# A graph kernel on one NeuronCore: setup work in another order, and entry groups two batches apart

## What is computed

```
h = relu(layernorm(x))
h = tanh(h @ W_in + b_in)
deg = clip(segment_sum(1, dst), 1)
for _ in range(12):
    agg = segment_sum(h[src], dst) / deg
    diff = tanh(gelu(agg @ W1 + b1) @ W2 + b2)
    h = h + (diff - relu(clearance) * h) * 0.5
x = x + h
h = relu(layernorm(x))
h = relu(gcn_conv(h, src + loops, dst + loops, G1, gb1))
x = x + gcn_conv(h, src + loops, dst + loops, G2, gb2)
```

## Time and profile before

| | |
|---|---|
| median of 3 runs | 1400.75 us (1399.76 to 1405.07) |
| the profiled execution | 1402.87 us |
| its span | 1400.7 us |
| mean granted clock | 0.965 |
| VectorE, ScalarE busy in the span | 405.4, 319.1 us |
| first regular window product, last one | 41.18, 152.93 us |
| first matmul of the edge sums | 156.66 us |

### The profile page before, as it was taken

The page is one execution under the profiler, slowest core; times in us unless marked ns, Lnnn a source line. Parts: engine busy times, 40 slices in busy tenths (PEclk is TensorE's granted clock), DMA queues, the critical chain, the costliest instruction groups (busy, mean ns, idle before and its releaser), DMA issues. The chain is left out here.

```text
span 1400.7 us, 17327 instructions
## 1 busy us (share of the span) xinstructions
PE 1305.5 (93%) x7202; PEld 737.1 (53%) x7202; DVE 405.4 (29%) x802; ACT 319.1 (23%) x452; POOL 34.5 (2%) x48
## 2 busy tenths in 40 slices
PE   2898899999999999999999999999999999759898
PEld 1777555455554554645546455454564555524445
DVE  6779412213022130121301213012130121382412
ACT  1678412213012130121301213012130121300100
POOL 3600000000000000000000000000000000000000
PEclk7689999999999999999999999999999999969999
DMA  3000200000000000000000000000000000130011
GB/s 92 1 1 0 59 1 0 0 0 0 0 0 0 0 0 0 0 0 0 0 0 0 0 0 0 0 0 0 0 0 0 0 0 0 46 92 1 20 43 31
DMA packets 23670, 13.57 MB, mean 10 GB/s; under 512 B 6075, under 2 KB 23253, under 8 KB 23392
## 3 DMA queue, kind: packets, MB, share of 16 engines
q1 hardware_dynamic: 21550, 12.28, 3.3%
q10 hardware_dynamic: 1698, 0.66, 0.2%
q0 software_dynamic: 400, 0.33, 0.1%
HBM read 9.42 MB, written 3.44 MB: 9 GB/s over the span
## 5 line engine op out<-in xcount | busy, mean ns | idle before, releaser
L619 PE MATMUL ps<-adj,hi 128*128 128x512 f16 (+2 forms) x2450 | 816.1, 354 | 29.9 <-DVE lo L1125 25.2
L621 PE MATMUL ps<-adj,lo 128*128 128x512 f16 (+2 forms) x2352 | 797.7, 353 | 0.0
L619 PEld LDWEIGHTS ps<-adj,hi 128*128 128x128 f16 x2450 | 238.6, 98 | 280.6 <-issue 46.5
L621 PEld LDWEIGHTS ps<-adj,lo 128*128 128x128 f16 x2352 | 229.6, 98 | 243.8 <-issue 24.2
L1040 DVE TENSOR_TENSOR ps<-ps,bias 128x512 f32<-128x512 f32 (+1 forms) x84 | 53.7, 640 | 547.9 <-PE ps L641 547.9
L782 ACT ACTIVATE scratch<-ps 128x512 f32<-128x512 f32 (+1 forms) x84 | 46.3, 551 | 655.4 <-DVE ps L1040 655.4
L632 PE MATMUL ps<-scratch,w 128*128 128x512 f32 (+2 forms) x336 | 141.0, 542 | 14.9 <-ACT scratch L774 14.9
L774 ACT ACTIVATE scratch<-ps,b1c,cols 128x512 f32<-128x512 f32 (+2 forms) x168 | 113.3, 721 | 156.9 <-PE ps L632 155.9
L641 PEld LDWEIGHTS ps<-w,scratch 128*128 128x128 f32 x1200 | 143.3, 192 | 6.3
L641 PE MATMUL ps<-w,scratch 128*128 128x128 f32 x1200 | 146.1, 275 | 0.0
L1033 DVE TENSOR_TENSOR scratch<-ps,scratch 128x512 f32<-128x512 f32 (+2 forms) x84 | 51.9, 618 | 189.8 <-PE ps L632 132.6
(11 more groups left out here) (123 smaller groups left out, 210.4 us busy)
## 6 DMA issues: line engine op xcount, KB each, us to landing
scratch<-rdeg_scratch SPq DMA_DIRECT2D x1, 1562.5 KB
scratch<-dinv_scratch SPq DMA_DIRECT2D x1, 1562.5 KB, 7.2
state<-in_x_dram SPq DMA_DIRECT2D x5, 256.0 KB, 6.7
scratch<-in_x_dram SPq DMA_DIRECT2D x5, 256.0 KB, 4.4
x_scratch<-state SPq DMA_DIRECT2D x5, 256.0 KB
state<-x_scratch SPq DMA_DIRECT2D x5, 256.0 KB
out_dram<-state SPq DMA_DIRECT2D x5, 256.0 KB
adj<-adj SPq DMA_DIRECT2D x1, 390.6 KB, 4.0
```

The costliest lines, as they stand in the source:

```text
L619: nc.tensor.matmul(bank, hi[:, k, :], adj[:, k, c0:c0 + n], start=(at == 0), stop=False)
L621: mm = nc.tensor.matmul(bank, lo[:, k, :], adj[:, k, c0:c0 + n], start=False, stop=(k == K_ORDER[-1][0]))
```

## The change

Four things are moved or rewritten. The packing and its stores go ahead of the choice operations and of the loads of x, and ScalarE's loads of the later weights wait for the stores; `clearance` gets a semaphore of its own, and TensorE waits for the weights ahead of the steps. The 12 chained scale operations become one scan. VectorE's key operations go between the statistics of the groups of x, and norm factors, steps and degrees go behind the one-hots of the first two batches. The ring has its transposes at batches 2, 4, ... 14, its products at 3, 5, ... 15, its `lo` at 7, 9, ... 19; 20 batches are unrolled instead of 32. The one-hots are laid out in runs of `RUN` = 2 windows instead of 4, with as many elements per operation.

```diff
+RUN = 2
+EVERY = 2
+TURN_AT = [2 + EVERY * g for g in range(NG)]
+PROD_AT = [b + EVERY // 2 for b in TURN_AT]
+LO_AT = [b + 4 for b in PROD_AT]
-ENTRY_BATCHES = 32
+ENTRY_BATCHES = (LO_AT[-1] + 2) // 2 * 2
...
-            Lb.append(half[:, o:o + nl].rearrange("p (b i w) -> p b i w", b=BANKS, w=BANK_WIN))
+            Lb.append(half[:, o:o + nl].rearrange("p (b i w) -> p b i w", b=BATCH // RUN, w=RUN))
...
-            for g in range(NG):
-                for sbuf, dram in rows(state, x, g):
-                    sp.dma_start(sbuf, dram).then_inc(s_x[g], 16)
             sp.wait_ge(s_packed, 1)
             p_v = packed_dram.rearrange("(p c) -> p c", c=CHUNK)
             sp.dma_start(p_v[0:112, :], packed[0:112, :]).then_inc(s_packed_out, 16)
             sp.dma_start(p_v[112:WQ, :], packed[112:WQ, :]).then_inc(s_packed_out, 16)
+            for g in range(NG):
+                for sbuf, dram in rows(state, x, g):
+                    sp.dma_start(sbuf, dram).then_inc(s_x[g], 16)
...
+            pe.wait_ge(s_w, 16 * 8)
...
+            act.wait_ge(s_packed_out, 32)
             act.dma_start(w1[:, :], W1).then_inc(s_w, 16)
...
-            link(V.memset(bound[:, 0:1], 2.0))
-            for t in range(STEPS):
-                link(V.tensor_scalar(bound[:, t + 1:t + 2], bound[:, t:t + 1], decay, 1.0 / (2 * DT),
-                                     ALU.mult, ALU.add))
+            V.memset(bound[:, 0:1], 2.0)
+            link(V.memset(pow2, 1.0 / (2 * DT)))
+            link(V.tensor_tensor_scan(bound[:, 1:STEPS + 1], decay.broadcast_to((128, STEPS)), pow2[:, 1:STEPS + 1], 2.0,
+                                      ALU.mult, ALU.add))
...
-            statistics(lambda g: dve.wait_ge(s_x[g], 16 * parts(g))).then_inc(s_var, 1)
...
+            for g in range(NG):
+                dve.wait_ge(s_x[g], 16 * parts(g))
+                last = row_statistics(g)
+                if g >= 2:
+                    key_fields(g - 2)
+                if 1 <= g <= WCOLS:
+                    key_group(g - 1)
+            link(last)
+            variances().then_inc(s_var, 1)
...
             for b in range(ENTRY_BATCHES):
+                dve.wait_ge(s_kc, min(b * BATCH + BATCH - 1, WINDOWS - 1) // WQ + 1)
                 batch(b % 2, b // 2)
                 if b == 0:
+                    norm_factors()
+                    degree_steps()
+                if b == 1:
+                    degrees()
+                if b == 2:
                     dve.wait_ge(s_degsum, 1)
...
-                if b % 4 == 2 and 1 <= b // 4 <= NG:
-                    split_lo(b // 4 - 1, b // 4, first_scale)
+                if b in LO_AT:
+                    split_lo(LO_AT.index(b), LO_AT.index(b) + 1, first_scale)
```

More of the change, by code:

```diff
@@ L832, in _ @@
             link(V.tensor_copy(chunk_d[:, 0:CHUNK + 1], e_in_d))
+            dve.wait_ge(s_src, 32)
+            V.scalar_tensor_tensor(out=packed, in0=e_in_d[:, 0:CHUNK], scalar=float(PACK), in1=e_in_s, op0=ALU.mult,
+                                   op1=ALU.add).then_inc(s_packed, 1)
             link(V.tensor_scalar(past, thresholds, chunk_d[:, CHUNK:CHUNK + 1], None, ALU.is_gt))
@@ L835, in _ @@
                                    ).then_inc(s_here, 1)
-            dve.wait_ge(s_src, 32)
-            V.scalar_tensor_tensor(out=packed, in0=e_in_d[:, 0:CHUNK], scalar=float(PACK), in1=e_in_s, op0=ALU.mult,
-                                   op1=ALU.add).then_inc(s_packed, 1)
             for g in range(WCOLS):
@@ L905, in _ @@
-            dve.wait_ge(s_kc, WCOLS)
-            for d in range(WIN + 1):
-                last = V.tensor_scalar(steps16[:, d, :], key_r, float(LANES * d + 1), None, ALU.is_ge)
-            last.then_inc(s_steps, 1)
-            dve.wait_ge(s_counted, 1)
-            sums = ps[0:WQ, 6, 0:WCOLS * (WIN + 1)].rearrange("p (g d) -> p g d", d=WIN + 1)
-            link(V.tensor_copy(root[0:WQ, :].rearrange("p (g d) -> p g d", d=WIN), sums[:, :, 1:WIN + 1]))
-            link(V.tensor_tensor(deg[0:WQ, :].rearrange("p (g d) -> p g d", d=WIN), sums[:, :, 0:WIN],
-                                 root[0:WQ, :].rearrange("p (g d) -> p g d", d=WIN), ALU.subtract))
@@ L914, in _, with degree_steps @@
-            V.tensor_reduce(deg_sum[0:WQ, :], deg[0:WQ, :], AX.X, ALU.add).then_inc(s_deg, 1)
+            for g in range(NG):
[7 more added lines that the diff above has]
+            variances().then_inc(s_var, 1)
+            def degree_steps():
+                dve.wait_ge(s_kc, WCOLS)
+                for d in range(WIN + 1):
+                    last_ = V.tensor_scalar(steps16[:, d, :], key_r, float(LANES * d + 1), None, ALU.is_ge)
+                last_.then_inc(s_steps, 1)
@@ new lines, in degrees @@
+            def degrees():
+                dve.wait_ge(s_counted, 1)
+                sums = ps[0:WQ, 6, 0:WCOLS * (WIN + 1)].rearrange("p (g d) -> p g d", d=WIN + 1)
+                link(V.tensor_copy(root[0:WQ, :].rearrange("p (g d) -> p g d", d=WIN), sums[:, :, 1:WIN + 1]))
+                link(V.tensor_tensor(deg[0:WQ, :].rearrange("p (g d) -> p g d", d=WIN), sums[:, :, 0:WIN],
+                                     root[0:WQ, :].rearrange("p (g d) -> p g d", d=WIN), ALU.subtract))
+                V.tensor_reduce(deg_sum[0:WQ, :], deg[0:WQ, :], AX.X, ALU.add).then_inc(s_deg, 1)
@@ L1103, in _ @@
             dve.wait_ge(s_x2, NG)
-            statistics(lambda g: None).then_inc(s_x2v, 1)
+            for g in range(NG):
+                last = row_statistics(g)
+            link(last)
+            variances().then_inc(s_x2v, 1)
             dve.wait_ge(s_x2s, 1)
```

80 lines of the change are left out of this document (40 added, 40 removed).

## The result

| | before | changed |
|---|---|---|
| median of the runs | 1400.75 us (1399.76 to 1405.07, 5 runs) | 1390.29 us (1389.93 to 1393.24, 5 runs) |
| ratio | | 0.9923 (0.9906 to 0.9939) |
| profiled execution: time, span | 1402.87, 1400.7 | 1393.24, 1391.4 |
| last regular window product starts | 152.93 | 142.50 |
| first edge sum starts | 156.66 | 145.69 |

The change is worth 10.5 us, or 0.77%: faster by more than the 0.5% that counts here. The time went where the prediction looked, ahead of the edge sums; but the setup and the ring each gave about five, where the ring was to give 0.7.

A forecast was written before the change was run, and what follows sets the result against it. TensorE is busy 93%, but the change acts in the first 157 us, where VectorE mostly sets the pace. Setup -5.05 and ring -0.7 made -5.7: 1395.1 us from a median of 1400.75, range 1389 to 1403.5.

The forecast's parts named there:

- Setup, steps 1 to 5: Before the ring: packing +1.0, stores ahead of x free, scan -2.7, keys between statistics, earlier counts; third product 5.05 us earlier.
- Ring, -0.7 said: Third window product to last regular one: 107.2 us instead of 107.9; -3.5 with no slow group, +6.5 with all five.
- One-hots in rows of two keep 0.875 an operation: VectorE's one-hots in the ring: rate unchanged, as operands still move in adjacent pairs; bounds 0.875 to 1.9.
- The plain pace: Ring's batches without groups: 35 at 1.80 make 63.0 us, plus 1.2 for the last lo operations.
- The groups: Ring's entry groups: first 7.97, 1.4 at 7.67 (half clock), 3.6 at 5.66, short one 3.9; 43.0 us for 14 batches.
- Closer groups save little work; they are only moved from a stretch bound by VectorE to one bound by TensorE: Ring: a group costs 2.06 over two plain batches instead of 2.4, or 4.1 instead of about 4.2 at half clock.
- A: Whole kernel: the sum, 1395.1 us, between 1393 and 1398 for 1 to 2 slow groups; chance 0.46.
- B, the clock holds: Ring's groups: TensorE, hardly ever idle, keeps its full clock; ring -3.5, in all -8.6, 1392.2 us; chance 0.25.
- C: Ring's groups: the clock stays low through all; ring +6.5, in all +1.5, 1402.3 us; chance 0.10.
- D, the one-hots lose their rate: VectorE's one-hots with rows of two take 1.9 at worst, 1.65 possibly, instead of 0.875; +81, 1482 us; chance 0.06.
- E, late data: Setup: x, started 5 us later, holds the statistics' merging 3 to 4; setup -1.5, 1399 us; chance 0.08.
- F, GpSimd starves: Ring's groups: GpSimd's row rescaling takes 2 us each, later transposes wait about 5 in all; 1400 us; chance 0.05.

The follow-up runs named there:

- alone 4.6 in time: Changed kernel with the ring as before (RUN 4, groups four batches apart, lo two behind): 1397.07 beside 1401.62, ratio 0.9967.
- the three kernels with the new setup and rows of four: New setup, RUN 4: groups per four with lo at +2 (0.9967) or +4 (0.9911), and groups per two with lo at +4 (0.994), against the kernel before.
- The kernel with rows of four: Changed kernel with RUN = 4 instead of 2, new setup and close groups kept: 1393.61 us, ratio 0.994 to the kernel before.
- the kernel with a group per four: Changed kernel with EVERY = 4 instead of 2, rows of two and lo at +4 kept: 1384.39 us, ratio 0.9877 to the kernel before.
- rows of one: Changed kernel with RUN = 1 instead of 2: 1465.7 us, one execution.
- rows of six: Changed kernel with RUN = 6 instead of 2: 1414.21 us, one execution.
- groups per five: Changed kernel with EVERY = 5 instead of 2: 1390.18 us, ratio 0.9902 to the kernel before.
- per three: Changed kernel with EVERY = 3 instead of 2: 1390.38 us, ratio 0.991 to the kernel before.

## Why the prediction was right, and where its sum was not

**Setup, steps 1 to 5: as said.** Third product 40.21 against 40.0, statistics at 18.71 against 18.0, steps' start 31.51 against 31.3. The packing cost more than said: with the cast ahead of it, which ended at 6.35 instead of 5.95, the scan's place moved by 1.3 instead of 1.0, inside the bounds. The late cast belongs to no term of the setup: it goes with the rows of two, through GpSimd's filling of the count tiles. The scan gave 2.8 (-2.7 said), x and the gathers were never waited for, the root was hidden under the one-hots. -4.8 against -5.05, and alone 4.6 in time. That the place came out within 0.25 is in part luck: in the three kernels with the new setup and rows of four it moved by 5.6 to 5.9, and the rows of two took about 1 of it back. Those three were near the end of their slack for the gathers: in two of them the keys waited 0.56 and 0.69 for the first.

**Ring, -0.7 said, -5.6 measured.** The kernel with rows of four parts the miss of 4.9. It has everything that the ring's sum priced, late lo and close groups, with windows of 1.56, and it gives -3.1 (104.8 instead of 107.9). So, by one profiled execution of each kernel, 2.4 of the miss are there without the new columns, and 2.5 came by them. The first half is mostly the first group, put at half clock throughout (below). The step that failed for the second half is the sentence "One-hots in rows of two keep 0.875 an operation": true, but written as if VectorE were the only reader of those tiles. TensorE reads them as operands, and for it the columns moved from 8 to 4 bytes apart. The price of twelve windows, taken from rows of before, was wrong for the kernel after: 1.02 instead of 1.56.

| us | said | rows of four | the change |
|---|---|---|---|
| seven groups, third product to the first plain batch | 43.0 | 41.5 | 41.1 |
| 35 batches to the last regular product, with the last lo | 64.2 | 63.3 | 61.2 |

- *The plain pace.* "35 batches at 1.80 = 63.0", with 1.2 for late lo. Measured, from 81.30 to 142.50: 61.2. Of the 3.0 less, 2.1 came by the columns. The prediction named VectorE as the bound of this stretch at 1.75, from 44 operations in 38.48, and beside it stood TensorE's 1.80. The last two of the 44 are the short ones of the window left over; the 42 before them took 37.74, so VectorE too ran at 1.80 a batch, and its own operations need only about 1.72 (0.86 from start to start, before as after). The difference was a wait for windows, about 0.14 in every second batch. With windows of 1.02 it is gone, and nothing interrupts VectorE's 1.72.
- *The groups.* "First group 7.97, 1.4 at 7.67, 3.6 at 5.66, the short one 3.9", together 43.0. Measured: 6.39, 6.33, 5.82, 5.52, 6.35, 6.49, 4.19, together 41.1, of which the columns gave only 0.4. The first group makes 1.6 of the difference: the clock rose inside it, at 45, and not behind it. The 7.67 never came, because where the clock fell it fell inside a group, for a product (68.79, 2.04) and the windows behind it, and not for all of it. Three of the next five groups met that, where 1.4 were forecast, at 0.8 to 1.0 each, where 2.0 were: two errors that cancel. At the full clock the 5.66 held with rows of four (5.68), and so did the cost over two plain batches, 2.08 against 2.06. With windows of 1.02 a group takes 5.52, bound by the loop through ScalarE and not by TensorE, as the step put it.

"Closer groups save little work; they are only moved from a stretch bound by VectorE to one bound by TensorE" was too kind. They cost 6.5 with rows of two and 4.1 with rows of four. The step counted a group over two plain batches, 2.06 against 2.4, and so never asked what a group costs when lo is late *and* the batches around it are four: by the kernel with a group per four, 0.8 (7.70 over four batches of 1.72), little more than lo itself. The gain of late lo (6.7 with rows of two, 7.8 with rows of four) and the loss by close groups (6.5 and 4.1) nearly cancel with rows of two and leave about 3.7 with rows of four. So the small ring term was right in its sign, but a balance of two large terms that the sum never saw.

**The rivals.** *A*, the sum, missed its own 1393 to 1398 by 2.7. *B, the clock holds*, did not come, though its time was the nearest of all (1392.2 said); that is luck. Windows of the changed kernel, columns as in the earlier trace rows:

```profile
59.80:66.60 6.80, 5.55 (x54) 4.38 (x52) 5.40 (x7) 5.82 (x7) 0.00 (x0) 1.00 0.01 4
...
76.90:90.50 13.60, 9.26 (x91) 7.73 (x90) 11.52 (x15) 10.60 (x12) 0.00 (x0) 0.88 0.01 2
```

The clock is full in the first, half in parts of 70 to 80 (granted 0.72 there), and not held by a TensorE that is "hardly ever idle": it idles more than before. *C* fell with it. *D, the one-hots lose their rate*: not at rows of two; shown to be real at rows of one. The Trainium skill, Vector Engine (DVE) Microarchitecture Reference, section 5.1, which asks for a step of one and more than one element innermost, agrees with both (0.86 at two, 1.65 at one). *E, late data*: no wait for x. *F, GpSimd starves*: its 25 operations ended at 53.9 and nothing waited for them:

```profile
31.70 22.20 POOL L492 TENSOR_SCALAR state<-state,cols 128x128 f32<-128x128 f32 x25 [11.91 <-DVE cols L932]
```

*After the ring nothing changes*: nearly. The edge sums begin 11.0 earlier, and in the changed kernel TensorE soon waits for a copy of a part of `adj`, which it did not in the kernel before, whose first edge sums ran at half clock (0.59 each instead of 0.38). Timeline of TensorE, changed kernel:

```profile
158.39 0.90 PE L628 MATMUL ps<-adj,hi 128*128 128x512 f16 x2 [2.59 <-DMA adj<-adj]
```

At the first convolution (1232.10 against 1242.71) 10.6 are left. The convolutions, where nothing was changed, took another 1.3 back in the profiled execution, the slowest of the changed kernel's five; by the medians 10.5 are left at the end.

## What to carry to other kernels

When a change alters a tile's layout, list every engine that reads or fills the tile, and price each one's work anew: rows of before hold for instruction counts, not for strides. Put work that needs another engine's answer (here lo, behind hi) so late that it finds the answer there, before packing anything closer; where it can be chosen, let it fall where its engine would wait for the next group (read from the rows of the group per four, not tried by itself). Before moving work into a denser stretch, write out the loop of answers that goes through all its engines; here its length (5.52), not any engine's busy time, set the distance between two groups.

## What the runs showed of the hardware that was not expected

TensorE's reads of f16 columns have a cost by distance: 12 windows (128 columns of weights, 125 of moving data) take 1.01 and 1.02 at 2 and 4 bytes, 1.56 at 8, 2.21 at 12 bytes at the full clock. The weight loads show it too (0.82 for 12 at 4 bytes, 1.27 at 8). The Trainium skill, Advanced Engine Details and Errata, section SBUF Cachelines, speaks of 16-byte lines on which two hits suffice. By it 8 bytes, with two columns to a line, would be as fast as 4, and a loss would begin at 12; the runs show half as much again at 8, and the measurement decides.

A cast of VectorE (0.38 alone) that began beside GpSimd's filling of the count tiles ended 0.23 to 0.26 behind it, after up to 2.60 (rows of six); the filling of 128x250 with rows of two took longer (1.88) than that of 128x500 with rows of four (1.37).

Executions of one kernel on one chip differ by 4.4 to 5.8 us (groups per five, per three, and the kernel before); for the first two the lowest time goes with the highest granted clock. A difference of 2 us between variants of this kernel can be placed by the trace, but was not proven by five runs.
